# Attention score stacks of even and odd heads in the two partition halves, four score banks and three ring banks

## The chip, the cores and the metric

The kernel runs on one core of a Trainium2 chip. The metric is the device time of one execution in microseconds. TensorE (PE) multiplies, VectorE (DVE), ScalarE (ACT) and GpSimd (POOL) work on what it leaves in PSUM and on SBUF, and SyncE (SP) issues most of the DMAs.

## The reference

One transformer layer on 16 sequences of 512 tokens with 256 channels, beside a context of 1601 rows per sequence:

```python
q = _heads(x @ Wq + bq); k = _heads(x @ Wk + bk); v = _heads(x @ Wv + bv)      # 16 heads of 16 channels
y = softmax(causal(q @ k.T * scale)) @ v                                          # own tokens
y = y + softmax(qc @ kc.T * scale) @ vc                                           # qc = x @ Wcq + bcq, kc and vc from the context
x = x + tanh(g_xattn) * (y @ Wp + bp)                                             # x was layer-normed on the way in
x = x + tanh(g_ffn) * (routed(x) + shared(x))                                     # 32 experts, 4 per token, and a shared one
```

`routed` sends each token to its four best experts (softmax of `x @ Wg`), each a SwiGLU of width 128; `shared` is a SwiGLU of width 256. All arrays are float32.

## The kernel before

**Stages.** `build_attention` goes over the 16 sequences, `build_experts` works through groups of 256 rows sent to one expert, and `build_merge` adds up. The change touches the first stage alone.

**Slots.** A sequence is cut into 68 slots (`SLOTS`), `slot_of(n)`: four quads `g` of four heads each, and in each quad 13 tiles of 128 context rows ("cross") and 4 of own tokens ("self"). In each slot PE makes the transposed scores of four heads, in two pairs (`scores`, L492), into the banks `scores` of PSUM, ACT takes their exponentials into `prob` (L688), and PE multiplies these by the values one slot later (`weighted`, L514), four heads side by side in strips of 32 columns of the array, into the bank `outs`. So PE's order in a slot is: scores of pair 0, items of the first half slot, scores of pair 1, items of the second half slot, outs of the slot before.

**Stacks.** Queries and keys are split into three bfloat16 parts each. A head's stack holds six products of parts below each other (`QP`, `KP`), 6 x 16 = 96 rows, and two more rows with the shift of the softmax (minus the row's maximum, against ones), 98 rows in all. One matmul of 98 rows by 512 columns makes the scores of a head for one tile.

**Maxima.** The shift needs each query's maximum over all keys before. PE makes the scores with queries in the partitions (item "cross", L570, 96 x 512; "rest", L577, four of 66 columns; "own", L586 with the causal mask added by L587), DVE takes the maximum of each (L882). These and all other results of the layer that pass PSUM (projections "split" and "value", "outproj", "router", "hidden", "shared", transposes, "shift") go through one ring of `RB` = 4 banks, in the order of the plan: `take` waits until the bank's last use has been read, `full` until the matmul is done. The maxima of a quad (64 per quad, 256 per sequence) are made while the quad before it is computed.

**The plan.** `plan(kind)` writes down which items stand in which of the 136 half slots. For a middle sequence (kind "M", 14 of the 16) a table `MAXIMA` says how many of the maxima stand in each half slot; elsewhere `fill` spreads them by costs. `BANKS` says how many banks of the ring an item takes. All engines follow the plan in its order; PE, DVE and ACT work strictly in order.

```python
RB, SB = 4, 3
pe.wait_ge(exped, part, before + 1)        # scores: the bank's exponential of SB heads ago
pe.wait_ge(freed[k], part, turn - 1)       # take: the ring bank's last use has been read
```

**DMA.** SP writes the parts to DRAM and reads each quad's stacks back (item "stack", L1266): six DMAs of 128 or 136 KB for each of three pieces, and two row DMAs (L1335) for each quad's shift.

## Time and profile before

| | |
|---|---|
| median of 3 runs | 4757.66 us (4754.53 to 4763.01) |
| span of the profiled execution | 4808.0 us |
| attention, 16 sequences | 120 to 4080 us of the span |
| experts and merge | 4080 to 4808 us |
| PE, DVE, ACT, POOL busy, share of the span | 90%, 73%, 56%, 34% |
| granted TensorE clock, mean | 0.962 |

The page gives no time of the profiled execution other than its span, which is 50.3 us (1.1%) longer than the median run. Busy time of PE counts a matmul until its result has landed; since the next one starts before that, the step from one matmul's start to the next one's tells what it costs. A float32 matmul shows as two records of half the length each. In the timeline "x4" is four records in a row, and the time beside it the stretch from the first start to the last end.

### The profile page before, as it was taken

To read this page: it belongs to the slowest core of one execution; us is meant where nothing else is said; L and a number is where in the kernel's file an instruction comes from. 1 tells how busy PE (TensorE), PEld (TensorE's weight loads), DVE (VectorE), ACT (ScalarE), POOL (GpSimd) and SP (SyncE) were. 2 spreads that over 40 slices of the span, in tenths; PEclk is the share of its full clock that TensorE was granted. 3 is DMA by queue.
4 is the path that set the end of the run, shared out by engine and by line. 5 is a ranking of instruction groups with operands and counts; after the bars stand their busy time and mean duration, and the time that the engine had idled before them with its cause. 6 is when DMAs were issued, how large, how long until landed. Compare 5 with 4: busy or idle time off the path is not lost. (4 is left out here: it accounts for less than half of the span.)

```text
span 4808.0 us, 75133 instructions
## 1 busy us (share of the span) xinstructions
PE 4323.8 (90%) x25317; PEld 1906.7 (40%) x25317; DVE 3532.5 (73%) x7733; ACT 2688.0 (56%) x5523; POOL 1651.4 (34%) x2163
## 2 busy tenths in 40 slices
PE   5999999999999999999999999999999995688882
PEld 2333333334343433333333333333333332577771
DVE  5788788888878787878788878788888783344443
ACT  1665656565656565665656565656665653344440
POOL 1122323232323232323232232323232314488883
PEclk7999999999999999999999999999999997899996
DMA  5443545454444344545444545454544444888888
GB/s 118 71 91 75 109 84 106 81 111 81 106 81 104 73 104 84 110 84 108 86 104 87 102 82 107 80 104 90 100 94 99 95 97 131 184 150 150 151 150 245
DMA packets 363501, 513.23 MB, mean 107 GB/s; under 512 B 64124, under 2 KB 227820, under 8 KB 363176
## 3 DMA queue, kind: packets, MB, share of 16 engines
q1 hardware_dynamic: 268240, 380.43, 38.0%
q0 software_dynamic: 87728, 115.39, 13.6%
q10 hardware_dynamic: 7208, 13.26, 0.9%
q8 instruction: 182, 2.98, 0.3%
q14 instruction: 143, 1.17, 0.1%
HBM read 288.49 MB, written 201.27 MB: 102 GB/s over the span
## 5 line engine op out<-in xcount | busy, mean ns | idle before, releaser
L688 ACT ACTIVATE prob<-scores 128x512 f32<-128x512 f32 (+3 forms) x4352 | 2141.6, 561 | 1268.5 <-PE scores L492 1251.6
L882 DVE TENSOR_REDUCE pmx<-ring 128x1 f32<-128x512 f32 (+1 forms) x3328 | 1999.1, 664 | 165.1 <-PE ring L570 158.3
L492 PE MATMUL scores<-stacks 98*128 98x512 bf16 (+3 forms) x4352 | 1291.0, 370 | 79.5 <-ACT prob L688 31.0
L514 PE MATMUL outs<-prob,vt 128*32 128x512 f32 x8704 | 1094.3, 575 | 4.9 <-POOL prob L1084 3.9
L570 PE MATMUL ring<-stacks 96*128 96x512 bf16 x3072 | 971.4, 389 | 64.1 <-DVE pmx L882 55.6
L492 PEld LDWEIGHTS scores<-stacks 98*128 98x128 bf16 (+1 forms) x4352 | 341.0, 99 | 1299.4 <-ACT prob L688 736.3
L1598 POOL DMA_INDIRECT scratch_sums<-e_yo,e_tok x320 | 496.3, 1551 | 116.7 <-issue 84.1
L882 DVE TENSOR_REDUCE mc<-ring 128x1 f32<-128x128 f32 (+3 forms) x1024 | 437.3, 483 | 123.1 <-PE ring L587 119.0
L1084 POOL TENSOR_SCALAR_AFFINE_SELECT prob<-prob 128x512 f32<-128x512 f32 x256 | 168.4, 658 | 1045.9 <-ACT prob L688 1036.0
L1154 POOL TENSOR_TENSOR split<-rest,split 128x512 bf16<-128x512 f32 (+1 forms) x224 | 218.8, 977 | 803.5 <-DVE split L976 803.0
L570 PEld LDWEIGHTS ring<-stacks 96*128 96x128 bf16 x3072 | 301.2, 99 | 450.9 <-DVE pmx L882 184.6
L1570 DVE TENSOR_SCALAR e_yo<-e_py,e_wcol 128x256 f32<-128x256 f32 x320 | 140.2, 480 | 284.4 <-DMA scratch_sums<-e_yo,e_tok 276.7
L973 DVE SCALAR_TENSOR_TENSOR rest<-ring,bcol,split 128x512 f32<-128x512 f32 (+1 forms) x224 | 153.2, 684 | 237.7 <-ACT split L722 233.9
L1472 PE MATMUL e_ph<-e_xt,e_we 128*128 128x256 f32 x1280 | 307.3, 383 | 4.3 <-ACT e_xt L1508 3.8
L514 PEld LDWEIGHTS outs<-prob,vt 128*32 128x32 f32 x8704 | 172.1, 108 | 338.8 <-issue 307.1
L586 PE MATMUL ring<-stacks 96*128 96x128 bf16 (+3 forms) x1024 | 259.4, 307 | 48.5 <-DVE mc L882 26.6
L1143 POOL DMA_INDIRECT scratch_slots<-split,rows x256 | 253.3, 989 | 92.4 <-issue 69.7
L1517 ACT COPY e_we<-stacks 128x768 f32 x160 | 133.2, 833 | 233.1 <-issue 143.5
L1472 PEld LDWEIGHTS e_ph<-e_xt,e_we 128*128 128x128 f32 x1280 | 240.6, 191 | 46.5 <-ACT e_xt L1508 11.3
L1481 PE MATMUL e_py<-e_we,e_act 128*128 128x256 f32 x640 | 179.0, 402 | 61.4 <-DVE e_act L1554 53.0
L722 ACT ACTIVATE split<-ring,bcol 128x512 bf16<-128x512 f32 (+1 forms) x224 | 142.3, 637 | 160.9 <-PE ring L541 109.9
L587 PE MATMUL ring<-maskb,identb 128*128 128x128 bf16 x1024 | 210.9, 223 | 0.0
(165 smaller groups left out, 3751.4 us busy)
## 6 DMA issues: line engine op xcount, KB each, us to landing
stacks<-scratch_parts SPq DMA_DIRECT2D x768, 128.0 KB, 7.2
stacks<-scratch_parts SPq DMA_DIRECT2D x384, 136.1 KB, 10.0
scratch_parts<-split SPq DMA_DIRECT2D x64, 768.0 KB, 4.5
e_xin<-scratch_slots SPq DMA_DIRECT2D x160, 289.0 KB
scratch_parts<-split SPq DMA_DIRECT2D x32, 816.8 KB, 4.5
num<-oc POOLq DMA_DIRECT2D x256, 64.0 KB
den<-scratch_inverses POOLq DMA_DIRECT2D x63, 256.0 KB, 8.4
ct<-in_ctx_t_dram SPq DMA_DIRECT2D x16, 800.5 KB, 8.1
```

The costliest lines, as they stand in the source:

```text
L492: eng.matmul(ps[0:m, k, q0:T], kst[g][0:KR + 2, j, k0:k0 + m], qst[g][0:KR + 2, j, qc + q0:qc + T], start=True, stop=True).then_inc(scored ...
L514: mm = eng.matmul(po[32 * j:32 * j + 32, q0:T], vt[ch][0:m, VW * vi + VE * hl:VW * vi + VE * hl + 32], prob[0:m, n % 2, j, q0:T], start=kt ...
L570: eng.matmul(dst, qst[g][0:KR, j, 128 * qt:128 * qt + 128], kst[g][0:KR, j, T + 512 * of:T + 512 * of + 512], start=True, stop=True).then_ ...
L586: eng.matmul(dst[:, 0:n], qst[g][0:KR, j, T + 128 * qt:T + n], kst[g][0:KR, j, 0:n], start=True, stop=False)
L587: eng.matmul(dst[:, 128 * qt:n], identb[:, :], maskb[:, :], start=False, stop=True).then_inc(ring.sem, 1)
L688: eng.activation(prob[0:m, n % 2, j, q0:T], ps[0:m, i % SB, q0:T], ACT.Exp, scale=SCALE).then_inc(exped.sem, 1)
L882: eng.tensor_reduce(dst, src, AX.X, ALU.max).then_inc(free_of(part, it), 1)
L1143: eng.indirect_dma_start(scr["slots"], bass.IndirectOffsetOnAxis(ap=rows[:, NQ * k + q:NQ * k + q + 1].bitcast(U32), axis=0), xs[:, ROW * ...
L1154: eng.tensor_tensor(last, rest[:, no % 2, 0:n], mid, ALU.subtract).then_inc(low.sem, 1)
L1472: op = eng.matmul(phd[i][:, m, :], we[g % UW][:, c0:c0 + H], xt[i][:, kc, :], start=kc == 0, stop=kc == KC - 1)
L1481: op = eng.matmul(py[i][:, q, :], act[i][:, 128 * q:128 * q + 128], we[g % UW][:, 2 * KC * H:], start=True, stop=True)
L1598: eng.indirect_dma_start(scr[f"sums{i}"], bass.IndirectOffsetOnAxis(ap=tok[u][:, q:q + 1].bitcast(U32), axis=0), yo[g % UO][:, q, :], None ...
```

## The change

**Stacks.** Each quad's stacks are split by head: even heads (of each of two pairs) lie in partitions 0 to 63, odd heads in 64 to 127, and each stack in two steps, one of four products (64 rows) and one of the last two products with the two shift rows (34 rows). A head's scores are now two matmuls that add up in one bank; the two heads of a pair alternate, each in its half of the array's rows.

**Maxima.** "cross", "rest" and "own" make the maxima of two heads side by side, from the first step's four products alone (the two smallest products are left out of the shift, which is the same for numerator and denominator). They take two banks. The causal mask is added in two matmuls of 64 rows per head.

**Banks and order.** Scores have four banks, the ring three. `MAXIMA` is gone and `fill` spreads the pairs by costs. Items that use the whole array stand only in second half slots, behind the maxima. **DMA.** Each stack DMA is split in two (one for each half), and each row DMA too.

```diff
-RB, SB = 4, 3
+RB, SB = 3, 4
...
 def max_items(g):
-    out = [("own", g, j, qt) for j in range(4) for qt in range(NQ)]
-    costs = [0.35 + 0.18 * qt for j in range(4) for qt in range(NQ)]
-    for j in range(4):
-        out += [("cross", g, j, qt, part) for qt in range(NQ) for part in range(3)] + [("rest", g, j)]
-        costs += [0.82] * (3 * NQ) + [0.46]
+
+    out = [("own", g, pair, qt) for pair in range(2) for qt in range(NQ)]
+    costs = [0.7 + 0.3 * qt for pair in range(2) for qt in range(NQ)]
+    for pair in range(2):
+        out += [("cross", g, pair, qt, part) for qt in range(NQ) for part in range(3)] + [("rest", g, pair)]
+        costs += [1.2] * (3 * NQ) + [0.8]
...
-MAXIMA = {
-    0: (5, 4, 1, 1, 4, 0, 1, 3, 2, 1, 3, 2, 4, 2, 2, 3, 2, 3, 2, 3, 2, 3, 3, 3, 3, 2, 2, 2),
...
-        if kind == "M":
-            for n, k in zip(range(lo, hi), MAXIMA[lo]):
-                out[n] += items[:k]
...
-    return [sorted(here, key=lambda it: it[0] in DEFERRED) for here in out]
+    for n, here in enumerate(out):
+        assert n % 2 or not any(it[0] in WHOLE_ARRAY for it in here)
+    return [sorted(here, key=lambda it: it[0] in WHOLE_ARRAY) for here in out]
...
-BANKS = {"trans": 1, "split": 1, "value": 1, "own": 1, "cross": 1, "rest": 1, "shift": 1, "outproj": 1, "router": 1,
+BANKS = {"trans": 1, "split": 1, "value": 1, "own": 2, "cross": 2, "rest": 2, "shift": 1, "outproj": 1, "router": 1,
...
-                for p in range(2):
-                    j, i = 2 * pair + p, 4 * n + 2 * pair + p
-                    k = i % SB
-                    before = i - SB if i >= SB else max(j for j in range(4 * SLOTS) if j % SB == k) - 4 * SLOTS
-                    pe.wait_ge(exped, part, before + 1)
-                    pe.wait_ge(rowed[g], part, row_no(g))
-                    eng.matmul(ps[0:m, k, q0:T], kst[g][0:KR + 2, j, k0:k0 + m],
-                               qst[g][0:KR + 2, j, qc + q0:qc + T], start=True, stop=True).then_inc(scored.sem, 1)
+                for step in range(2):
+                    for side in range(2):
+                        i = 4 * n + 2 * pair + side
+                        k = i % SB
+                        before = i - SB if i >= SB else max(j for j in range(4 * SLOTS) if j % SB == k) - 4 * SLOTS
+                        pe.wait_ge(exped, part, before + 1)
+                        pe.wait_ge(rowed[g], part, row_no(g))
+                        on = slice(64 * side, 64 * side + (SR + 2 if step else PR))
+                        mm = eng.matmul(ps[0:m, k, q0:T], kst[g][step][on, pair, k0:k0 + m],
+                                        qst[g][step][on, pair, qc + q0:qc + T], start=step == 0, stop=step == 1)
+                        if step:
+                            mm.then_inc(scored.sem, 1)
...
                 elif what == "cross":
-                    g, j, qt, of = it[1:]
-                    dst = take(part, it)
+                    g, pair, qt, of = it[1:]
                     pe.wait_ge(stacked_rest[g], part, load_no(part, g))
-                    eng.matmul(dst, qst[g][0:KR, j, 128 * qt:128 * qt + 128],
-                               kst[g][0:KR, j, T + 512 * of:T + 512 * of + 512], start=True, stop=True).then_inc(ring.sem, 1)
+                    for side in range(2):
+                        dst = take(part, it, side)
+                        on = slice(64 * side, 64 * side + PR)
+                        eng.matmul(dst, qst[g][0][on, pair, 128 * qt:128 * qt + 128],
+                                   kst[g][0][on, pair, T + 512 * of:T + 512 * of + 512], start=True, stop=True).then_inc(ring.sem, 1)
...
-                    for r, src in enumerate(parts):
-                        eng.dma_start(dst[g][D * r:D * r + D, :, c0:c0 + cn],
-                                      scr["parts"][ch, PIECES.index(kind), src][64 * v:64 * v + 64, 0:cn].rearrange(
-                                          "(h d) c -> d h c", d=D)).then_inc(done[g].sem, 16)
+                    for step, (lo, hi) in enumerate(STEPS):
+                        for r in range(lo, hi):
+                            src = scr["parts"][ch, PIECES.index(kind), parts[r]][64 * v:64 * v + 64, 0:cn].rearrange(
+                                "(p s d) c -> s d p c", p=2, s=2)
+                            for side in range(2):
+                                at = 64 * side + D * (r - lo)
+                                eng.dma_start(dst[g][step][at:at + D, :, c0:c0 + cn], src[side]).then_inc(done[g].sem, 16)
```

The order of PE moves with the plan. First a stretch in which a middle sequence has only scores, maxima and outs. L492 is the scores, L570 the cross maxima, L514 the outs ("x4" is four matmuls). Before:

```order
L492 MATMUL scores<-stacks 128x512 x2
L570 MATMUL ring<-stacks 128x512 x2
L492 MATMUL scores<-stacks 128x512 x2
L570 MATMUL ring<-stacks 128x512 x3
L514 MATMUL outs<-prob,vt 32x512 x4
```

The same stretch in the change (L485 the scores, L567 the cross maxima, L509 the outs):

```order
L485 MATMUL scores<-stacks 128x512 x4
L567 MATMUL ring<-stacks 128x512 x4
L485 MATMUL scores<-stacks 128x512 x4
L567 MATMUL ring<-stacks 128x512 x2
L509 MATMUL outs<-prob,vt 32x512 x4
```

A slot had five maxima here and has six now, in pairs; of the scores there are twice as many matmuls.

Second, the second half of a sequence's plan, where PE also makes the projections for the next one (L541 before and L536 now is a "split", a whole-array float32 product). Before:

```order
L541 MATMUL ring<-xt,wcq 128x512 x2
L514 MATMUL outs<-prob,vt 32x512 x4
L492 MATMUL scores<-stacks 65x512 x2
L570 MATMUL ring<-stacks 128x512 x4
L492 MATMUL scores<-stacks 65x512 x2
L514 MATMUL outs<-prob,vt 32x512 x4
L492 MATMUL scores<-stacks 128x512 x2
L570 MATMUL ring<-stacks 128x512 x2
L541 MATMUL ring<-xt,wq 128x512 x2
L492 MATMUL scores<-stacks 128x512 x2
L577 MATMUL ring<-stacks 128x66 x4
L514 MATMUL outs<-prob,vt 32x512 x4
```

In the change:

```order
L536 MATMUL ring<-xt,wcq 128x512 x2
L509 MATMUL outs<-prob,vt 32x512 x4
L485 MATMUL scores<-stacks 65x512 x4
L567 MATMUL ring<-stacks 128x512 x4
L485 MATMUL scores<-stacks 65x512 x4
L567 MATMUL ring<-stacks 128x512 x2
L509 MATMUL outs<-prob,vt 32x512 x4
L485 MATMUL scores<-stacks 128x512 x4
L567 MATMUL ring<-stacks 128x512 x2
L576 MATMUL ring<-stacks 128x66 x8
L485 MATMUL scores<-stacks 128x512 x4
L536 MATMUL ring<-xt,wq 128x512 x2
```

The split of `wq` stood in a first half slot, between two groups of scores; it now stands in the second, right ahead of the outs, and the maxima of its slot have all moved ahead of it.

## Rows read from the trace of the kernel before

**Rows 1.** The page: engines' busy time, then the costliest groups of part 5.

```profile
PE 4323.8 (90%) x25317; PEld 1906.7 (40%) x25317; DVE 3532.5 (73%) x7733; ACT 2688.0 (56%) x5523; POOL 1651.4 (34%) x2163
L492 PE MATMUL scores<-stacks 98*128 98x512 bf16 (+3 forms) x4352 | 1291.0, 370 | 79.5 <-ACT prob L688 31.0
```

**Rows 2.** Windows: start, length, PE, PEld, DVE, ACT, POOL busy (x), PEclk, DMA, GB/s.

```profile
120.00:4080.00 3960.00, 3725.40 (x22523) 1445.96 (x22521) 3162.99 (x6771) 2378.69 (x4857) 1130.84 (x1789) 0.98 0.46 94
1900.16:2144.74 244.58, 233.65 (x1424) 91.26 (x1423) 200.46 (x430) 149.65 (x306) 72.07 (x114) 0.99 0.46 95
```

**Rows 3.** Timeline of PE and DVE, a stretch of maxima: start, length, what.

```profile
1846.37 13.02 DVE L882 TENSOR_REDUCE pmx<-ring 128x1 f32<-128x512 f32 x22
1850.03 0.60 PE L492 MATMUL scores<-stacks 98*128 98x512 bf16 x2
1850.47 0.60 PE L570 MATMUL ring<-stacks 96*128 96x512 bf16 x2
1851.34 0.82 PE L570 MATMUL ring<-stacks 96*128 96x512 bf16 x3
1852.09 1.06 PE L514 MATMUL outs<-prob,vt 128*32 128x512 f32 x8
1853.08 0.61 PE L492 MATMUL scores<-stacks 98*128 98x512 bf16 x2
1854.74 0.38 PE L570 MATMUL ring<-stacks 96*128 96x512 bf16 x1
1855.05 1.07 PE L514 MATMUL outs<-prob,vt 128*32 128x512 f32 x8
```

**Rows 4.** Timeline of PE and DVE: waits of one for the other.

```profile
1881.76 3.27 DVE L882 TENSOR_REDUCE mc<-ring 128x1 f32<-128x128 f32 x8
1882.10 0.23 PE L586 MATMUL ring<-stacks 96*128 96x128 bf16 x1 [1.34 <-DVE mc L882]
1896.34 0.82 PE L570 MATMUL ring<-stacks 96*128 96x512 bf16 x2
1896.98 1.29 DVE L882 TENSOR_REDUCE pmx<-ring 128x1 f32<-128x512 f32 x2 [1.75 <-PE ring L570]
```

**Rows 5.** Groups by line, 1500 to 2500 us.

```profile
L882 DVE TENSOR_REDUCE pmx<-ring 128x1 f32<-128x512 f32 (+1 forms) x840 | 505.1, 663 | 45.8 <-PE ring L570 44.0
L882 DVE TENSOR_REDUCE mc<-ring 128x1 f32<-128x128 f32 (+3 forms) x256 | 109.7, 483 | 29.2 <-PE ring L587 28.2
```

**Rows 6.** Waits, 1500 to 2500 us: us in total, times, longest.

```profile
PEld ring L570 <- DVE pmx L882: 40.2, 95, 3.3
PE ring L570 <- DVE pmx L882: 12.4, 17, 3.0
PE scores L492 <- issue: 7.9, 8, 1.5
PE scores L492 <- ACT prob L688: 7.4, 19, 0.8
DVE rest L973 <- ACT split L722: 56.5, 44, 2.5
```

**Rows 7.** Timeline of PE: whole-array products beside the narrow outs.

```profile
1906.21 3.60 PE L616 MATMUL ring<-xt,ws 128*128 128x512 f32 x8
2019.68 0.43 PE L514 MATMUL outs<-prob,vt 128*32 128x128 f32 x8
2020.04 0.60 PE L492 MATMUL scores<-stacks 98*128 98x512 bf16 x2
```

**Rows 8.** Timeline of SP: stack and row DMAs.

```profile
1977.14 9.53 SPq L1266 DMA_DIRECT2D stacks<-scratch_parts  x18
2070.97 1.15 SPq L1335 DMA_DIRECT2D stacks<-mr  x2
```

**Rows 9.** Windows around a fall of the granted clock.

```profile
1879.00:1883.00 4.00, 2.53 (x25) 1.17 (x26) 3.76 (x15) 0.89 (x4) 0.86 (x5) 1.00 0.00 0
1887.00:1891.00 4.00, 4.00 (x18) 1.14 (x16) 3.08 (x5) 2.14 (x5) 0.00 (x0) 0.50 0.00 0
```

More of the change, by code:

```diff
@@ L572, in item @@
                 elif what == "rest":
-                    g, j = it[1:]
-                    dst = take(part, it)
+                    g, pair = it[1:]
                     pe.wait_ge(stacked_rest[g], part, load_no(part, g))
+                    dsts = [take(part, it, side) for side in range(2)]
                     for qt in range(NQ):
-                        mm = eng.matmul(dst[:, 66 * qt:66 * qt + 66], qst[g][0:KR, j, 128 * qt:128 * qt + 128],
-                                        kst[g][0:KR, j, T + TC - 66:T + TC], start=True, stop=True)
-                        if qt == NQ - 1:
-                            mm.then_inc(ring.sem, 1)
+                        for side in range(2):
+                            on = slice(64 * side, 64 * side + PR)
+                            mm = eng.matmul(dsts[side][:, 66 * qt:66 * qt + 66], qst[g][0][on, pair, 128 * qt:128 * qt + 128],
+                                            kst[g][0][on, pair, T + TC - 66:T + TC], start=True, stop=True)
+                            if qt == NQ - 1:
+                                mm.then_inc(ring.sem, 1)
@@ L581, in item @@
                 elif what == "own":
-                    g, j, qt = it[1:]
+                    g, pair, qt = it[1:]
                     n = 128 * (qt + 1)
-                    dst = take(part, it)
                     pe.wait_ge(stacked[g], part, load_no(part, g))
-                    eng.matmul(dst[:, 0:n], qst[g][0:KR, j, T + 128 * qt:T + n], kst[g][0:KR, j, 0:n], start=True, stop=False)
-                    eng.matmul(dst[:, 128 * qt:n], identb[:, :], maskb[:, :], start=False, stop=True).then_inc(ring.sem, 1)
+                    dsts = [take(part, it, side) for side in range(2)]
@@ new lines, in item @@
+                    for side in range(2):
+                        on = slice(64 * side, 64 * side + PR)
+                        eng.matmul(dsts[side][:, 0:n], qst[g][0][on, pair, T + 128 * qt:T + n], kst[g][0][on, pair, 0:n],
+                                   start=True, stop=False)
+                    for half in range(2):
+                        for side in range(2):
+                            on = slice(64 * side, 64 * side + 64)
+                            mm = eng.matmul(dsts[side][:, n - 128 + 64 * half:n], identb[on, 64 - 64 * half:192 - 64 * half], maskb[on, 0:128 - 64 * half],
+                                            start=False, stop=half == 1)
+                            if half:
+                                mm.then_inc(ring.sem, 1)
@@ L872, in item @@
                 elif what in ("cross", "rest", "own"):
-                    g, j = it[1:3]
-                    full(dve, part, it)
-                    src = pm[:, bank_of(part, it), :]
-                    if what == "cross":
-                        dst = pmx[:, j, it[3], it[4]:it[4] + 1]
-                    elif what == "rest":
-                        dst, src = pmx[:, j, :, 3], src[:, 0:66 * NQ].rearrange("p (q n) -> p q n", q=NQ)
-                    else:
-                        dst, src = mc[g % 2][:, 8 * j + 4 + it[3]:8 * j + 5 + it[3]], src[:, 0:128 * (it[3] + 1)]
-                    eng.tensor_reduce(dst, src, AX.X, ALU.max).then_inc(free_of(part, it), 1)
+                    g, pair = it[1:3]
+                    for side in range(2):
+                        full(dve, part, it, side)
+                        src, at = pm[:, bank_of(part, it, side), :], 2 * side + pair
+                        if what == "cross":
+                            dst = pmx[:, at, it[3], it[4]:it[4] + 1]
+                        elif what == "rest":
+                            dst, src = pmx[:, at, :, 3], src[:, 0:66 * NQ].rearrange("p (q n) -> p q n", q=NQ)
+                        else:
+                            dst, src = mc[g % 2][:, 8 * at + 4 + it[3]:8 * at + 5 + it[3]], src[:, 0:128 * (it[3] + 1)]
+                        eng.tensor_reduce(dst, src, AX.X, ALU.max).then_inc(free_of(part, it, side), 1)
                 elif what == "whole":
@@ L885, in item @@
                     for last in max_items(g)[0][-RB:]:
-                        read(dve, part, last)
+                        for side in range(2):
+                            read(dve, part, last, side)
                     eng.tensor_reduce(mc[g % 2][:, :].rearrange("p (h a q) -> p h a q", a=2, q=NQ)[:, :, 0, :], pmx[:, :, :, :],
@@ L1334, in second @@
                     for i in range(2):
-                        eng.dma_start(qst[g][KR + i:KR + i + 1, :, :].rearrange("o t c -> o (t c)"), mr[:, i, :]
-                                      ).then_inc(rowed[g].sem, 16)
+                        for side in range(2):
+                            at = 64 * side + SR + i
+                            eng.dma_start(qst[g][1][at:at + 1, :, :].rearrange("o t c -> o (t c)"), mr[16 * side:16 * side + 16, i, :]
+                                          ).then_inc(rowed[g].sem, 16)
                 elif what == "shared" and it[1] == NQ - 1:
```

72 lines of the change are left out of this document (39 added, 33 removed), and 3 rows, old and new, of the table MAXIMA.

## The prediction

> **What bounds the kernel now.** I read the page first. PE is busy for 90% of the span, DVE for 73%, ACT for 56% [rows 1]. The window of the attention stage says the same of 3960 us: PE 3725, DVE 3163 [rows 2]. One sequence (from one load of its input by SP to the next) takes 244.6 us, with DVE busy for 200.5 and ACT for 149.7 [rows 2]. But PE's busy time counts each matmul until it lands: a score matmul's record lasts 0.37 us [rows 1], while two of them step by 0.44 us, 0.22 each [rows 3]. So the timeline decides. From 1850.03 to 1853.08, a slot with five maxima takes 3.05 us [rows 3]. Its PE steps: four scores and five maxima at 0.22 are 1.98; a step of 0.31 instead of 0.22 where the outs begin (1854.74 to 1855.05) adds 0.09; the outs take 1.0 (1852.09 to 1853.08). Sum 3.07: PE waits for nothing. In the same stretch DVE makes 22 reductions in 13.02 us, 0.59 each, one behind the other [rows 3]: five in 2.95 us. So PE and DVE bind together, and four ring banks are just deep enough that neither notices the other.
>
> **What PE saves.** A sequence has 192 cross maxima (16 heads, 12 each) of 0.22 us. Two side by side, if they run at once, take the time of one: 96 x 0.22 = 21 us less. The 64 own ones average 320 columns, 0.13 us: 4 us less; their masks (0.06 each) become four narrow matmuls a pair, which I take as even. Scores are even: two matmuls of one head each become two steps of two heads each, 0.44 us a pair either way, if the halves overlap. No row shows two halves of the rows at work at once. The nearest are the outs, in strips of columns: eight records of 512 columns in 1.0 us [rows 3], where eight on the whole array last 3.60 us [rows 7]. I take a pair at 0.22 us, the bound from below; from above it is 0.44, two in turn.
>
> **What it costs PE.** 128 columns of outs take 0.36 us (2019.68 to 2020.04) [rows 7], 512 take 1.0 [rows 3]: 0.64 for 384 columns, so 128 cost 0.21 and 0.15 stay fixed; with the 0.09 ahead, changing between the whole array and strips costs about 0.1 each way. In the new plan 35 of 68 slots hold whole-array items between half-array scores and the outs, one more change each: 35 x 0.1 = 3.5 us, in the slot lengths below. The Trainium skill, TensorEngine Tiling (Array Packing), Key Properties, says that a change of tiling mode drains the engine; the fixed part of the outs agrees.
>
> **What the ring costs.** This is the term that decides. A pair takes two of three banks, so the second matmul of the second pair waits for the first reduction. From issue to issue that is 0.38 us until the matmul lands [rows 3], a handover (0.82 - 0.22 = 0.60 after 1896.34 it had landed, DVE began 0.04 later), 0.66 for the reduction [rows 5], and a handover back (PE began 0.34 after the start of the narrowest reduction, 128 columns; I take 0.06) [rows 4]: 1.13 us. Behind the last maximum of a slot PE is away for 0.31 + 1.0 + 0.44 (outs, next scores) = 1.75 us [rows 3], then 0.41 until DVE has something: 2.16. DVE has three banks to work off, at most 1.8. With four banks it had 2.4.
>
> Slots of the new plan, full width, W standing for their whole-array items:
> - 11 slots with a pair in each half: 1.13 + 1.75 = 2.88 us. Before, four maxima: 2.85.
> - 18 slots with three pairs: the sixth matmul waits for the third reduction, 0.41 + 1.2 + 0.66 + 0.06 = 2.33, and 1.75: 4.08. Before, six: 3.3 by PE, 3.6 by DVE.
> - 14 with two pairs and W behind them: 0.44 + 1.13 + 0.22 + 0.44 + 0.2 + 1.0 + W = 3.43 + W. Before: 2.85 + W.
> - 14 with one pair and W: 2.3 + W. Before, two maxima: 2.4 + W.
> - 3 at 2.99 + W, 2 at 4.19 + W, 2 at 2.08 + W, four others 11.4 together.
>
> Sum without W: 31.7 + 73.4 + 48.0 + 32.2 + 9.0 + 8.4 + 4.2 + 11.4 = 218.3. Own maxima are narrower, 0.43 against 0.60 [rows 5], 64 of them; not all lie where the ring binds, so I take off 8: 210. The same sum for before, PE's steps alone: 68 x 1.97 for scores and outs, 42 for cross, 3.4 for rest, 12.5 for own with masks: 192. So 18 more. From this goes what before already waits: for the ring between 12.4 and 40.2 us of 1000 (PE's own wait and that of its weight loads) [rows 6], at 4.09 sequences 3 to 10 us each; I take 8. The fourth score bank takes up to (7.9 + 7.4) / 4.09 = 3.7 us of waits for ACT [rows 6]; I take 3. A split keeps its bank and DVE while ACT works (56.5 us of 1000 in which DVE waits, 14 us a sequence [rows 6]); with a bank less, some of it now holds up the next slot: 2 more. 18 - 8 - 3 + 2 = 9 us a sequence. Its ends are 2 (own 11, ring waits 10, splits 0) and 18.
>
> **What costs nothing.** Stack DMAs double in number, not in bytes. SP issues 18 in 9.53 us [rows 8]; 36 would take 19, ahead of maxima that come about 30 us later. Row DMAs take 1.15 us for two [rows 8], now 2.3 for four, with six half slots in hand. If that cover goes, the first scores of a quad wait a microsecond, 4 a sequence, within the range. DVE, ACT and POOL keep their work. Experts and merge don't change.
>
> **Sum.** 16 x 9 = 149 us (9.3 unrounded). On the profiled execution 4808 becomes 4957; the median run is 50.3 us shorter, and I put the forecast on it: 4757.66 + 149 = 4907 us. Its own range, from 2 and 18 us a sequence: 4790 to 5050.
>
> **Rivals.**
> - **The halved maxima carry** (faster): the deciding point is whether DVE keeps work while PE is in the outs; its other work (200.5 busy, of which maxima are 614.8 / 4.09 = 150 [rows 2, 5]) would have to fall into the gaps. Then PE needs 21 + 4 + 3 - 3.5 = 25 us less, but DVE's 200.5 and its 14 of waits for ACT leave 215 at least. 244.6 - 25 = 220: 4757.66 - 16 x 25 = 4358; with half of it lost, 4560. For it speaks PE's 90%, against it the 100% of DVE in rows 3. The Trainium skill's page TensorEngine Tiling (Array Packing), Theoretical Speedup, gives up to twofold for contractions of 64 or less, which would be this case; its Restrictions and Gotchas name PSUM pressure of row tiles, which would be my forecast.
> - **No change** within 0.2%: both cancel, 4748 to 4767.
> - **The clock** (slower still): after 1.34 us without work in rows 4 the granted clock fell from 2.4 to 1.2 GHz (0.50 at 1887 us [rows 9]). PE has more such holes now, though shorter ones of up to 0.7 us. A four-maxima slot of 2.85 us would take about 5 at 1.2 GHz, for its outs and scores double. If a further 5 to 10% of the 3960 us ran so, and a third to a half of that were lost, 70 to 200 us come on top: 4980 to 5110.
> - **The halves don't overlap** (the change doesn't do what it says): scores double, 272 x 0.22 = 60 us a sequence, 16 x 60 = 960, and the maxima save nothing: about 5700. Against it the strips of the outs.
>
> **Chances.** Forecast 0.60; clock 0.08; no overlap 0.03; no change 0.05; the halved maxima carry, in whole or in part, 0.24. So slower by over 0.2% (about what a measurement here can tell) 0.71, same 0.05, faster 0.24. The range reaches down into the partial gain, 4570, and up to 5090; about one in five is left out, most of it below.
>
> **What would show it.** Right: starts of the two cross matmuls of a first pair 0.01 to 0.05 us apart, of a second pair over 0.5 apart with "DVE pmx" as releaser; slots with two pairs near 2.9 us and with three near 4.1; DVE's idle time for ring matmuls, 44.0 + 28.2 in 1000 us now [rows 5], up to over 110; waits of scores for ACT gone; PE's idle time up. A sequence near 254 us. Wrong: DVE busy above 85% of the stage, a sequence under 240 us, or three-pair slots under 3.7. Score matmuls stepping by 0.22 each instead of in twos would mean no overlap.

## The result, and the profile after

The changed kernel takes 5421.61 us (median of 4 runs, 5410.17 to 5435.31). The kernel before, run beside it, takes 4760.34 (4754.53 to 4766.18). The ratio is 1.139, its 95% interval 1.1368 to 1.1411: 661 us slower, where 149 slower was forecast, and outside the range. The sign and the place were right, the size was not.

The profiled execution has a span of 5433.2 us (before 4808). The page, engines and the costliest groups (busy us, mean ns, idle time ahead and what ended it):

```profile
PE 4495.8 (83%) x30693; PEld 1828.3 (34%) x30693; DVE 3561.6 (66%) x7733; ACT 2689.2 (49%) x5523; POOL 1640.9 (30%) x2168
...
L892 DVE TENSOR_REDUCE pmx<-ring 128x1 f32<-128x512 f32 (+1 forms) x3328 | 1997.8, 661 | 415.2 <-PE ring L567 412.1
L485 PE MATMUL scores<-stacks 64*128 64x512 bf16 (+1 forms) x8704 | 1362.0, 383 | 22.4 <-DMA stacks<-mr 22.3
L567 PE MATMUL ring<-stacks 64*128 64x512 bf16 x3072 | 927.0, 399 | 318.1 <-DVE pmx L892 273.4
...
L892 DVE TENSOR_REDUCE mc<-ring 128x1 f32<-128x128 f32 (+3 forms) x1024 | 451.5, 485 | 278.8 <-PE ring L592 278.6
...
L587 PE MATMUL ring<-stacks 64*128 64x128 bf16 (+3 forms) x1024 | 176.8, 334 | 186.1 <-DVE mc L892 167.4
```

DVE has the same work as before (3532.5 us then [rows 1], 3561.6 now), and one reduction takes the same 661 ns. Neither engine has more to do; both stand still more. DVE waits for PE's maxima, and PE waits for DVE's.

The windows (start, length, busy time of PE, PEld, DVE, ACT, POOL with counts, granted clock, DMA share, GB/s), first the attention stage, then one sequence from SP's load of its input to the next:

```profile
120.00:4700.00 4580.00, 3890.54 (x27898) 1366.16 (x27899) 3194.78 (x6781) 2382.23 (x4861) 1117.55 (x1787) 0.93 0.31 82
2180.95:2467.58 286.63, 244.84 (x1766) 85.10 (x1758) 202.54 (x430) 149.58 (x306) 71.71 (x115) 0.94 0.33 82
```

The stage is 620 us longer than the 3960 of [rows 2], and the two profiled executions differ by 625, so all of the loss lies there. A sequence took 244.6 us in [rows 2] and takes 284 to 290 in four of the change, with a mean of 287.0. That 244.6 was one of the shortest: over all 14 middle sequences, from first scores to first scores, the mean was 247.0 (244.7 to 252.0) and is 288.4 (285.2 to 293.8), 41.4 more. DVE's 202.5 and ACT's 149.6 stand against 200.5 and 149.7 before. The granted clock fell from 0.98 to 0.93.

A slot with three pairs of cross maxima, in the timeline of PE (start, length, what, idle time ahead):

```profile
2123.78 0.61 PE L485 MATMUL scores<-stacks 64*128 64x512 bf16 x4
2124.22 0.38 PE L567 MATMUL ring<-stacks 64*128 64x512 bf16 x2
2124.45 0.59 PE L485 MATMUL scores<-stacks 64*128 64x512 bf16 x4
2124.88 0.90 PE L567 MATMUL ring<-stacks 64*128 64x512 bf16 x2
2125.99 0.39 PE L567 MATMUL ring<-stacks 64*128 64x512 bf16 x1 [0.21 <-DVE pmx L892]
2126.58 0.39 PE L567 MATMUL ring<-stacks 64*128 64x512 bf16 x1 [0.21 <-DVE pmx L892]
2126.90 1.06 PE L509 MATMUL outs<-prob,vt 128*32 128x512 f32 x8
2127.90 0.61 PE L485 MATMUL scores<-stacks 64*128 64x512 bf16 x4
```

Four score matmuls pass in 0.44 us (2123.78 to 2124.22), and the two maxima of the first pair have one record of 0.38: the halves work at once, as the sum assumed. The second pair's record lasts 0.90, so its matmuls are 0.52 apart. Those of the third pair come one by one, 0.59 apart, at the rate of DVE's reductions. The slot takes 4.12 us; the forecast was 4.08.

The table of waits between 1500 and 2500 us (total us, times, longest):

```profile
DVE pmx L892 <- PE ring L567: 92.4, 107, 2.9
DVE mc L892 <- PE ring L592: 64.8, 90, 4.9
PE ring L567 <- DVE pmx L892: 59.1, 157, 3.7
PE ring L587 <- DVE mc L892: 37.2, 56, 2.1
PEld scores L485 <- ACT prob L696: 65.6, 84, 1.3
DVE rest L984 <- ACT split L730: 71.8, 47, 4.3
```

DVE's idle time for ring matmuls is 157 us of 1000, where it was 44.0 + 28.2 [rows 5]. PE's own wait for DVE was 12.4 [rows 6] and is 59.1; that ahead of the own maxima was 6.7 and is 37.2.

**Where the slots differ from the plain pattern.** Slots in which DVE has other work between the reductions show larger holes. The timeline of PE and DVE in one of them, where DVE makes the statistics of the next sequence's input:

```profile
2200.70 1.29 DVE L892 TENSOR_REDUCE pmx<-ring 128x1 f32<-128x512 f32 x2 [0.99 <-PE ring L567]
...
2201.90 1.40 DVE L804 BATCH_NORM_STATS2 stat<-xa 128x6 f32<-128x256 f32 x4
...
2202.76 0.61 PE L485 MATMUL scores<-stacks 64*128 64x512 bf16 x4
2203.33 0.38 DVE L807 BATCH_NORM_AGGREGATE mv<-stat 128x2 f32<-128x6 f32 x4
...
2204.03 2.56 DVE L892 TENSOR_REDUCE pmx<-ring 128x1 f32<-128x512 f32 x5
...
2204.86 0.31 PE L576 MATMUL ring<-stacks 64*128 64x66 bf16 x8 [1.49 <-DVE pmx L892]
```

DVE's reductions resume only at 2204.03. PE needs two free banks for its next pair and stands for 1.49 us. Then DVE works off what there is and waits for the next pair.

### The profile page after: what moved, and what is told of

The parts are those of the page before. It is cut to its first block and busy times, and to the rows that moved or that the text cites. A ratio compares the mean times of both kernels' runs of the same rounds, so it can differ in the third digit from the quotient of the medians.

```text
span 5433.2 us, 87801 instructions
## 1 busy us (share of the span) xinstructions
PE 4495.8 (83%) x30693; PEld 1828.3 (34%) x30693; DVE 3561.6 (66%) x7733; ACT 2689.2 (49%) x5523; POOL 1640.9 (30%) x2168
## 5 line engine op out<-in xcount | busy, mean ns | idle before, releaser
L485 PE MATMUL scores<-stacks 64*128 64x512 bf16 (+1 forms) x8704 | 1362.0, 383 | 22.4 <-DMA stacks<-mr 22.3
L567 PE MATMUL ring<-stacks 64*128 64x512 bf16 x3072 | 927.0, 399 | 318.1 <-DVE pmx L892 273.4
L509 PE MATMUL outs<-prob,vt 128*32 128x512 f32 x8704 | 1157.0, 606 | 14.6 <-POOL prob L1095 14.6
L485 PEld LDWEIGHTS scores<-stacks 64*128 64x128 bf16 (+1 forms) x8704 | 336.9, 98 | 1096.4 <-issue 651.2
L892 DVE TENSOR_REDUCE mc<-ring 128x1 f32<-128x128 f32 (+3 forms) x1024 | 451.5, 485 | 278.8 <-PE ring L592 278.6
L567 PEld LDWEIGHTS ring<-stacks 64*128 64x128 bf16 x3072 | 236.3, 98 | 943.8 <-DVE pmx L892 742.4
L984 DVE SCALAR_TENSOR_TENSOR rest<-ring,bcol,split 128x512 f32<-128x512 f32 (+1 forms) x224 | 153.3, 684 | 344.4 <-ACT split L730 343.2
L587 PE MATMUL ring<-stacks 64*128 64x128 bf16 (+3 forms) x1024 | 176.8, 334 | 186.1 <-DVE mc L892 167.4
L509 PEld LDWEIGHTS outs<-prob,vt 128*32 128x32 f32 x8704 | 176.1, 111 | 357.9 <-issue 291.9
L558 PE MATMUL ring<-wcv,ct 128*128 128x128 f32 (+1 forms) x832 | 150.0, 330 | 7.3 <-DVE rest L984 4.0
```

The source lines that it names most:

```text
L485: mm = eng.matmul(ps[0:m, k, q0:T], kst[g][step][on, pair, k0:k0 + m], qst[g][step][on, pair, qc + q0:qc + T], start=step == 0, stop=step ...
L509: mm = eng.matmul(po[32 * j:32 * j + 32, q0:T], vt[ch][0:m, VW * vi + VE * hl:VW * vi + VE * hl + 32], prob[0:m, n % 2, j, q0:T], start=kt ...
L567: eng.matmul(dst, qst[g][0][on, pair, 128 * qt:128 * qt + 128], kst[g][0][on, pair, T + 512 * of:T + 512 * of + 512], start=True, stop=Tru ...
L587: eng.matmul(dsts[side][:, 0:n], qst[g][0][on, pair, T + 128 * qt:T + n], kst[g][0][on, pair, 0:n], start=True, stop=False)
L892: eng.tensor_reduce(dst, src, AX.X, ALU.max).then_inc(free_of(part, it, side), 1)
```

## The experiments

A ratio is to the kernel before, run beside each, with its 95% interval. The kernel before took 4756 to 4815 us from one set of runs to the next, 1.2% apart: about 4810 beside e1 to e4 and e9 to e11, about 4760 beside the change and the others. No run shows whether the changed kernel varies in the same way. So where two rows with different neighbours are compared and differ by little, both ratios and medians are given, and a difference that only one of them shows is not shown.

| label | edit | median us | ratio |
|---|---|---|---|
| e1 | change, ring 4, scores 3 | 5172.88 | 1.076 (1.0732 to 1.0788) |
| e2 | before, ring 3, scores 4 | 5146.29 | 1.070 (1.067 to 1.0731) |
| e3 | change, ring 5, scores 2 | 5480.36 | 1.1394 (1.1365 to 1.1423) |
| e4 | change, half-width reductions | 5092.12 | 1.0606 (1.0565 to 1.0646) |
| e5 | change, outs in mid-slot | 5589.72 | 1.1748 (1.1722 to 1.1774) |
| e6 | e5 with ring 4, scores 3 | 5209.59 | 1.0948 (1.0925 to 1.0971) |
| e7 | before with the change's plan | 4831.01 | 1.0154 (1.0132 to 1.0175) |
| e8 | change, extra matmuls | 5423.49 | 1.1402 (1.1371 to 1.1432) |
| e9 | change, banks taken singly | 5397.78 | 1.1196 (1.1165 to 1.1228) |
| e10 | e9 with ring 4, scores 3 | 5181.54 | 1.0758 (1.0739 to 1.0776) |
| e11 | e10, before's places | 5176.19 | 1.0747 (1.0729 to 1.0765) |
| e12 | before, scores wait per pair | 4831.43 | 1.0147 (1.0118 to 1.0176) |
| e13 | e1, second pair in turn | 5089.21 | 1.0697 (1.0668 to 1.0727) |

### The ring's fourth bank given back

```diff
-RB, SB = 3, 4
+RB, SB = 4, 3
```

> The change with its banks put back: four for the ring, three for scores; all else as in the change. Theory A, the ring of three binds (two and three pairs in a slot at 2.92 and 4.12 us in the change's trace, and the ends of slots with other DVE work): the loss goes, two-pair slots fall to about 2.45 us, three-pair slots to 3.6, a sequence to 225 to 240 us, the median to 4450 to 4700, below the kernel before. Theory B, the row halves, the doubled DMAs or the plan without the table of maxima cost the time: the median stays over 5100. Theory C, the granted clock (618 us at half speed against 130) falls because of the half-array matmuls themselves: the time at half speed stays over 400 us here too.

Measured: 1.076, a sequence 269.4 us. Going back to four ring banks returns less than half of the loss, and the median lies above the 5100 that theory B named; e7 and the DMA waits below take the plan and the DMAs out of question as its main cause. The three-pair slots went from 4.12 to between 3.52 and 3.61 us, but the slots with a pair in each half rose from 2.92 to 3.05. Theory C is refuted: with the same half-array matmuls the time at the lower clock in the attention stage falls from 682 to 340 us (e8 has the counts of the change and of before). So a part of what this run returns is the clock and not the slots. The timeline of PE shows what holds them:

```profile
2007.48 0.61 PE L485 MATMUL scores<-stacks 64*128 64x512 bf16 x4
2007.93 0.38 PE L567 MATMUL ring<-stacks 64*128 64x512 bf16 x2
2008.15 0.37 PE L485 MATMUL scores<-stacks 64*128 64x512 bf16 x1
2008.78 0.60 PE L485 MATMUL scores<-stacks 64*128 64x512 bf16 x3 [0.25 <-ACT prob L696]
...
2011.07 0.61 PE L485 MATMUL scores<-stacks 64*128 64x512 bf16 x4
```

With three score banks the second pair has one free bank. Its first matmul starts at 2008.15, the next 0.63 us later, when ACT has finished with head 0. The pair takes 0.86 us until the maxima follow at 2009.01, where it took 0.44. In a slot with three pairs DVE is the slower one and hides that (six reductions at 0.6 are 3.6). In the others it shows: a pair in each half 3.05 where 2.45 was expected, and one pair with a split 4.74 where the change has 4.10. So part of the wait only moved from the ring to the scores, for the page says of these:

```profile
L892 DVE TENSOR_REDUCE pmx<-ring 128x1 f32<-128x512 f32 (+1 forms) x3328 | 1985.4, 662 | 295.7 <-PE ring L567 257.5
L485 PE MATMUL scores<-stacks 64*128 64x512 bf16 (+1 forms) x8704 | 1638.4, 375 | 231.1 <-ACT prob L696 186.9
```

### A ring of three in the kernel before

```diff
-RB, SB = 4, 3
+RB, SB = 3, 4
```

> The kernel before with three ring banks and four for scores; stacks, plan and maxima of single heads stay. Theory A: a slot with five maxima waits for the second reduction and takes 3.5 us instead of 3.05, one with six 4.1 instead of 3.27; with the other places the median comes to 5100 to 5450 us, and the time at half clock rises to several hundred us. Theory B: within 1% of 4760.

Measured: 1.070. A ring of three alone, without pairs and with heads of 98 rows, costs 7%. Slots with five maxima take 3.52 us; with six they take 3.86 where one is a rest item and 4.12 where all are cross; a sequence takes 266 to 271. DVE's idle time for PE in the page:

```profile
L882 DVE TENSOR_REDUCE pmx<-ring 128x1 f32<-128x512 f32 (+1 forms) x3328 | 2010.7, 663 | 325.0 <-PE ring L570 316.6
```

This is half of the change's loss. The time at the lower clock is 259 us in the stage (177 before), so here nearly all of the loss is in slots at full clock.

### Five banks for the ring, two for the scores

```diff
-RB, SB = 3, 4
+RB, SB = 5, 2
```

> The change with five ring banks and two for scores. Theory A says the ring alone would be no limit any more (DVE's idle time for ring matmuls under 40 us of 1000), but each pair of scores now waits for both exponentials of the pair before, 0.41 + 2 x 0.54 us behind them: a two-pair slot at 3.2 to 3.5 us, the median 4700 to 5100. If scores' banks mattered little: under 4600. Theory B: over 5100.

Measured: 1.1394, as slow as the change (the median is 1% above it), and above what was expected. The ring hardly holds PE up any more, the scores do (the page):

```profile
L485 PE MATMUL scores<-stacks 64*128 64x512 bf16 (+1 forms) x8704 | 1697.8, 377 | 513.4 <-ACT prob L696 395.5
L567 PE MATMUL ring<-stacks 64*128 64x512 bf16 x3072 | 711.4, 392 | 40.3 <-DVE pmx L892 38.3
```

DVE's idle time for ring matmuls stays at 79.3 + 42.6 us of 1000, where under 40 was expected, because PE now comes late from the scores. Of seven banks, three, four and five for the ring give 1.139, 1.076 and 1.139: none of the three divisions serves both pools.

### Reductions over half the columns

```diff
-dst = pmx[:, at, it[3], it[4]:it[4] + 1]
+dst, src = pmx[:, at, it[3], it[4]:it[4] + 1], src[:, 0:256]
```

The maxima of the context part leave out half of the keys here.

> The change with each cross maximum taken over 256 of its 512 columns, which leaves half of the keys out of the shift; PE's work is the same. A reduction falls by 0.27 us. Theory A: two-pair slots fall by one reduction to 2.65 us, three-pair slots by three to 3.3, a sequence by 25 to 40 us, the median to 4750 to 5000. If PE's own work on the row halves were the bound (theory B): both slots as in the change, the median over 5300.

Measured: 1.0606. A reduction takes 418 ns in place of 661; a slot with a pair in each half went from 2.92 to 2.66 and one with three pairs from 4.12 to 3.32. That agrees with a chain of steps with the reduction in it. But a sequence fell only to between 262 and 272 (mean 267), and the median stayed above the range expected. DVE has 786 us less work (the page: 2775.8 against 3561.6), yet this beats the change by 6 to 7% only (medians and ratios), and is still slower than before. So halving the reduction does not take away what is left.

### The outs in the middle of the slot

```diff
-                    if n or not part.first:
-                        weighted(part, n - 1)
+                        if pair == 0 and (n or not part.first):
+                            weighted(part, n - 1)
```

The call moves from behind both pairs into the loop, behind the first half slot's items.

> The change (ring three, scores four) with PE's outs of the slot before moved from the slot's end to behind the first half slot's items. Theory A, what PE does behind the last maximum of a group decides: the outs now lie while the third bank of a pair is being reduced, so three-pair slots fall from 4.12 to about 3.65 us (DVE's six reductions). Two-pair slots can't fall below 2.76, since exponentials of the second pair (0.63 + 1.08 us behind its scores) must end before the outs: 2.8 against 2.92. Slots with two pairs and a whole-array item stay. Median 5100 to 5300. Theory C, the clock, adds that fewer holes lift the granted clock above 0.919. If the order didn't matter: 5420.

Measured: 1.1748, worse than the change, where better was expected. The timeline of PE shows a slot behind a split:

```profile
2000.19 0.38 PE L567 MATMUL ring<-stacks 64*128 64x512 bf16 x2
2001.36 0.39 PE L567 MATMUL ring<-stacks 64*128 64x512 bf16 x1 [0.80 <-DVE rest L984]
2002.42 0.39 PE L567 MATMUL ring<-stacks 64*128 64x512 bf16 x1 [0.67 <-DVE pmx L892]
```

In the change's plan the outs follow the whole-array items and cover the time in which ACT and DVE work on a split. Without them the next pair comes too early and DVE stands at L984 (114.7 us of 1000, where the change has 71.8). The slots with two pairs and a split rise from 5.28 to 5.91 us, while three-pair slots take 3.4 to 4.7, most of them no more than the 4.12 of the change. So the gap of 1.75 us behind the maxima is only part of the price there, and moving it costs more in the slots with a split.

With `RB, SB = 4, 3` as well:

> The same with four ring banks and three for scores. Against the run with ring four and scores three alone (5173): the second pair's scores no longer wait for the exponential of the first pair's first head, because the outs lie between; the next slot's first pair waits instead (0.5 us where only one pair of maxima lies between). Two-pair slots 2.85 to 2.95, three-pair 3.6, median 4900 to 5150. If the wait only changes its place: 5150 to 5200.

Measured: 1.0948, again worse than with the outs at the end (e1, 1.076; medians 5209.59 and 5172.88), and above both ranges.

### The new plan alone

```diff
-DEFERRED = ("split", "value", "shift", "outproj", "hidden", "shared")
+WHOLE_ARRAY = ("trans", "split", "value", "shift", "outproj", "router", "hidden", "shared", "rank")
...
-        if kind == "M":
-            for n, k in zip(range(lo, hi), MAXIMA[lo]):
...
-        deal(0, (57, 60, 63, 66, 69, 72, 75), split_items(0), 1.8)
+        deal(0, (57, 61, 63, 67, 69, 73, 75), split_items(0), 1.8)
```

> The kernel before (single heads on the whole array, ring four, scores three) with the change's placing: no table of maxima, the new places of the whole-array items, these last in second half slots only. If the plan is no part of the loss: within 1% of the kernel before. If it is a part (theory D: the order of the items had been set so that waits of 0.2 to 3 us at slots with other DVE work did not arise): 2 to 5% slower, 4900 to 5050, and some of what is left in the run with ring four and scores three is the plan's.

Measured: 1.0154, between the two expectations. The order of the work costs 1.5% in the kernel before, so it is a small part of the 13.9%.

### Extra matmuls ahead of the own and rest maxima

```diff
-                    dsts = [take(part, it, side) for side in range(2)]
+                    dsts = [take(part, it, 0)]
+                    for _ in range(2):
+                        eng.matmul(dsts[0], qst[g][0][0:PR, pair, T:T + 128], kst[g][0][0:PR, pair, 0:512], start=True, stop=True)
+                    dsts += [take(part, it, 1)]
```

Two more of 512 columns for each pair of own maxima and four for each pair of rest, 96 a sequence, overwritten by what follows. At 0.22 us each they are 21 us a sequence, 336 in all.

> The change with work added where PE waits for DVE: in each own pair two, in each rest pair four further matmuls of 64 rows by 512 columns into the pair's first bank, which the real ones then overwrite: 96 a sequence, 21 us if none lay in a hole. Theory C, the half-speed stretches (618 us against 130) carry 200 us or so of the loss: the time at half speed falls below 350 us and the median stays or falls, 5250 to 5450, in spite of the added work. If the clock is worth nothing: the median rises by 100 to 300 us.

Measured: 1.1402, no change, with 336 us more for PE to do. The trace's clock records show 461 us of the attention stage (120 to 4700 us) at 1.2 GHz, where the change has 682 and the kernel before (120 to 4080 us) 177. That is less of a fall than was expected. PE's idle time went from 42 to 26 us a sequence, so most of the added work lies in what were pauses. Two slots tell the price of the lower level, since nearly the same work stands there at both. The first has four of the added matmuls at the higher level, so its difference is put low; the second has none. Windows of the changed kernel, then of this one:

```profile
2247.72:2252.91 5.19, 4.58 (x34) 1.68 (x30) 1.96 (x5) 1.58 (x5) 0.63 (x1) 0.50 0.00 0
2377.23:2382.71 5.48, 5.48 (x24) 1.29 (x21) 1.22 (x3) 3.06 (x7) 0.63 (x1) 0.50 0.40 64
```

```profile
2252.79:2256.31 3.52, 3.43 (x38) 1.34 (x35) 1.78 (x4) 1.35 (x5) 0.64 (x1) 1.00 0.01 1
2379.48:2382.40 2.92, 2.92 (x23) 0.86 (x20) 0.28 (x2) 2.79 (x7) 0.59 (x1) 1.00 0.99 135
```

5.19 us against 3.52, and 5.48 against 2.92: 32 and 47% of the time at the lower level is lost. The change has 682 - 177 = 505 us more of it, so 160 to 240 us are lost (an estimate from two slots). Ahead of the first of these stretches PE stood for 0.50 and 0.86 us (the changed kernel's timeline):

```profile
2244.91 0.39 PE L587 MATMUL ring<-stacks 64*128 64x512 bf16 x2 [0.50 <-DVE mc L892]
...
2246.24 0.23 PE L587 MATMUL ring<-stacks 64*128 64x128 bf16 x2 [0.86 <-DVE mc L892]
```

The Trainium skill, TensorE: Matmul & The Clock Gate, in the section on a second failure mode by cycling of the PSUM queue, describes a kernel whose clock swings between the two levels because of short pauses between groups of matmuls. The trace agrees in part: before it has 30 stretches at the lower level in this stage, now 113. But not every short pause brought one. In slots 5 to 13, 25 to 31 and 51 to 63 PE stands for 0.2 us ahead of many of the cross maxima and for up to 0.9 ahead of rest items, and in none of the 14 middle sequences does a lower stretch start there. They start in 15 other slots, most of these around the own maxima, the routing and the next input's statistics, and most stretches have a pause of 0.5 to 3.4 us close ahead of them.

### Banks taken one after the other

```diff
-                    dsts = [take(part, it, side) for side in range(2)]
+                    for side in range(2):
+                        dst = take(part, it, side)
+                        on = slice(64 * side, 64 * side + PR)
```

The own and rest maxima of the second head start once its own bank is free, and don't hold back the first head's. The cross maxima did so already.

> The change (ring three), but own and rest items take their two banks one after the other: side 0 is multiplied as soon as one bank is free, and the two sides no longer overlap. Theory A2, pairs that wait for two banks at once leave DVE empty (64.8 us of 1000 in which DVE waits for a mask matmul, holes of 1.5 and 1.8 us ahead of rest items): DVE's wait for L592 falls below 40 us of 1000, some falls of the clock go with it, the median 5200 to 5350. If overlap of the two sides were worth more than the earlier start: above 5420.

Measured: 1.1196, above the range expected. How much better than the change this is stays open: by ratios 1.7% (93 us), by medians 0.4% (24 us), and the attention stage of its trace is 45 us shorter. DVE's wait for the own maxima falls from 64.8 to 47.9 us of 1000, not below 40. So waiting for both banks at once costs somewhere between 24 and 93 us net of the overlap of the halves, which is given up here for these items.

> The same with four ring banks and three for scores. With four banks two are mostly free together, so it should change little against 5173: 5130 to 5190. If it falls by over 100, pairs also block a ring of four.

Measured: 1.0758, the same as e1. With four banks the second one is free anyhow.

```diff
-WHOLE_ARRAY = ("trans", "split", "value", "shift", "outproj", "router", "hidden", "shared", "rank")
+DEFERRED = ("split", "value", "shift", "outproj", "hidden", "shared")
...
-        deal(HALF, (47, 51, 53, 57, 59, 63, 65), split_items(1), 1.8)
+        deal(HALF, range(47, 66, 3), split_items(1), 1.8)
```

> As the run before, with the whole-array items at the kernel before's places (first half slots too) and its sorting; the maxima still spread by costs. Theory D (the plan): the kernel before lost 1.5% by the new places, so this gains 1 to 2%, 5050 to 5130. Theory E: what is left against the kernel before (5173 to 4760) is the pairs of scores on three banks, where the second pair stops for 0.63 us until the first head's exponential is done; then the old places change under 1% here, and waits of scores for ACT stay near 187 us.

Measured: 1.0747, the same (medians 5181.54 and 5176.19). The places of the whole-array items don't matter here.

### The wait for a pair of score banks in the kernel before

```diff
-pe.wait_ge(exped, part, before + 1)
+pe.wait_ge(exped, part, before + 2 - p)
```

> The kernel before, with one wait made longer: the first score matmul of a pair waits not only for its own bank's exponential but for that of the pair's second head as well, as interleaved pairs on three banks must. Nothing else differs. Theory E (what is left with ring four is this wait): second pairs stop until the first head's exponential is done, 0.4 to 0.6 us in slots with one to two maxima between, 5000 to 5200. If the wait is hidden by ACT's slack (60% busy): within 1% of the kernel before.

Measured: 1.0147, far less than expected. A slot with five maxima takes 3.27 us in place of 3.05 where two stand in the first half, and 3.05 where three do. The stop is 0.22 with two maxima between the scores and 0.42 with one. In e1 the pair of scores loses 0.42 (0.86 in place of 0.44) with two maxima between: a pair of maxima takes PE only as long as one, which is 0.22, and a head's scores land 0.60 us after their start, in two steps, where they landed after 0.38 in one, which is 0.22 again. So the wait alone does not explain e1; the later landing and the shorter maxima each count as much (worked out from the timelines, not separated by a run).

### The second pair of scores head after head

```diff
 RB, SB = 4, 3
...
-                for step in range(2):
-                    for side in range(2):
+                for step, side in ((0, 0), (1, 0), (0, 1), (1, 1)) if pair else ((0, 0), (0, 1), (1, 0), (1, 1)):
+                    for _ in range(1):
```

> Ring four, scores three, but in the second pair of a slot first both steps of one head, then both of the other, without overlap: the first head's scores no longer wait for the second head's bank, but the pair takes 0.88 us of PE instead of 0.44. Theory E: the stop of 0.63 us turns into work of 0.44: two-pair slots 2.9 instead of 3.05, those with a wait gone (three maxima between) slower; 5100 to 5200. If PE's steps, not ACT, were the limit there: 5173 + 16 x 68 x 0.44 = 5650.

Measured: 1.0697, a sequence 262.7 us. Slots with a pair in each half take 3.05 us and those with two pairs and a split 4.74, both as in e1. The timeline of PE in a slot with a pair in each half:

```profile
2043.78 0.61 PE L485 MATMUL scores<-stacks 64*128 64x512 bf16 x4
2044.22 0.38 PE L567 MATMUL ring<-stacks 64*128 64x512 bf16 x2
2044.44 1.01 PE L485 MATMUL scores<-stacks 64*128 64x512 bf16 x3
...
2045.82 1.07 PE L509 MATMUL outs<-prob,vt 128*32 128x512 f32 x8
```

PE works 0.88 us on the second pair (four steps of 0.22) where it worked 0.44 and stood 0.42. It stands nowhere in this slot, so here its own steps fill the 3.05 us, and in e1 nearly the same sum comes from work and a stop. With three score banks the overlap of this pair is worth nothing: what it saves turns into a wait for ACT. Against e1 the gain is 0.6% by ratios, 1.6% by medians and 6 us a sequence in the traces, part of it from fewer stretches at the lower clock (clock 0.955 against 0.948).

## Why the prediction was right and wrong

**Overlap of the halves: right.** A pair costs 0.22 us, and four score steps of 512 columns 0.44.

**Cover of the DMAs: right.** The first scores of a quad wait 22.3 us in all for their row DMAs, 1.4 a sequence (between 1500 and 2500 us 6.7, where it was 3.5). DVE's and ACT's work is unchanged.

**Slot lengths: right.** Forecast against measured, at the full clock: a pair in each half 2.88 and 2.92; three pairs 4.08 and 4.12; two pairs and a split of 1.8 us 5.23 and 5.28; one pair and a split 4.1 and 4.10. Summed over the 68 slots these steps give 229.5 us for before and 245.9 now (my sum, no run shows it as such), 16.4 a sequence where the text had 18: 262 us over 16 sequences. The traces fit it roughly: in slots 5 to 13, 25 to 31 and 51 to 63, the plain stretches of the plan, a sequence takes 16.2 us more than before, some 2 of which are whole-array items that the new plan moved there (an estimate).

**The step that failed: "18 - 8 - 3 + 2 = 9".** I took off the ring waits and waits for ACT that the kernel before had, as if longer slots would swallow them. But those waits are not in the plain slots. They stand where DVE has other work (statistics, routing, splits), where the ring runs dry for a moment. There a bank less, and own and rest pairs that want two, made them grow. What a sequence takes above its steps was 247.0 - 229.5 = 17.5 us and is 288.4 - 245.9 = 42.5. The term was 25 with a plus in place of 9 with a minus. The other 39 slots show it without that sum: together they take 25.2 us more. And a bank less alone, without pairs, costs the kernel before 22 us a sequence (e2, 268.9 against 247.0), where ring and pairs together were put at 9. The waits for ACT did shrink (65.6 us of 1000 at the weight load, where the kernel before has 178.2), but that bought little, since PE's own wait there had been 7.4.

**The clock: a rival that came on top.** It was put at 0.08 and as an alternative. Its condition, 5 to 10% of the 3960 us more at 1.2 GHz, was exceeded (505 us is 13%), and its price came out at the upper end of the stated 70 to 200 us or above it. It did not come from the plain slots, whose waits the working has and which brought no lower stretch; it came with the pauses at DVE's other work and the own maxima, the same places as the failed step. So of some 660 us, 262 are the ring in plain slots as computed, 160 to 240 the clock, and some 160 to 240 waits at DVE's other work. The two traces give this split another way. The shortest passage of each of the 68 slots in the 14 middle sequences adds up to 238.2 us before and 268.3 now, 30.1 more: 16.4 of these are the steps, and the other 13.7 (219 us over 16 sequences) are waits that are there every time. What a mean sequence takes above that was 8.8 and is 20.1, 11.3 more (181 us), most of it in slots that a lower stretch touches. Slots that are never free of one keep some of its cost in the first part. Of the waits, e9 puts 24 to 93 us down to two banks at once. No run separated the clock from the waits.

**The halved maxima carry: refuted for this ring and for others.** Even with four banks (e1, e10, e11, e13) the change stays 7 to 7.6% behind. The 25 us of PE's time are saved by the working, but where the ring has three banks the slot is set by hand-overs to DVE, and where the scores have three or two by hand-overs to ACT; in e13, which gives up half of the overlap of the scores, PE's steps fill the slot again. Theory A, that the ring of three explains nearly all, fell with e1: its removal gives back 1.139 - 1.076, less than half, and some of that is the clock. In its place: pairs want two banks at once from both pools. In the three divisions that were run seven banks serve only one of them, and the other then stops PE, or, where the cross maxima take what is free one by one, the pair no longer runs side by side. How the 7.6% of e1 divides is open: e7 and e12 put 1.5% each on the plan and on the wait in the kernel before, and no run has the stacks in two steps without the pairs.

**Expected signs.** First pair's starts close together: seen. Second pair's over 0.5 apart with DVE as releaser: seen (0.52 to 0.59). Slots 2.9 and 4.1: seen. DVE idle over 110 us of 1000: 157. A sequence near 254: missed, 287 to 288. No experiment beat the kernel before. Not tried: four banks for each pool, one more than the seven that the two pools have here.

## What to carry to other kernels

Running two matmuls side by side in the halves of the array saves PE time only if the readers can take two results at once: count the free banks of each pool at the instant of the second take, not on average. Waits that a kernel already has cannot be netted against a new bound unless they lie in the same slots; look at which slots they stand in, above all those where the draining engine has other work. When a change lengthens the pauses of a nearly busy PE, price the lower clock as part of the forecast and not as a rival to it, and do so where the pauses are long: here the pauses in the plain slots, 0.2 us mostly and 0.9 at single places, brought no lower stretch, and most of those that came had pauses of 0.5 to 3.4 us close ahead.

## What the runs showed of the hardware

Four matmuls of 64 rows by 512 columns, two in each half of the array, start the next work 0.44 us after the first (2123.78 to 2124.22), and two such maxima have a joint record of 0.38. The price of a two-step product is in its landing: 0.60 us after the start in place of 0.38 [rows 3], which was 0.22 of the 0.42 that a pair of scores lost in e1. Adding 336 us of matmuls to PE changed the time by nothing measurable (1.139 and 1.1402): 221 us less were spent at 1.2 GHz, and PE's idle time fell from 42 to 26 us a sequence. At the lower level a slot lost 32 to 47% of its time, not half. DVE and ACT kept their speed: in the changed kernel's trace a 512-column reduction takes 0.68 us at either level and an exponential 0.60, where a 64-row matmul of 512 columns has a record of 0.61 us in place of 0.38.
